# A two-layer transformer kernel: another split of its head's fills, loads and waits, and identity turns on PE at four seams

## The chip, the cores and the metric

The kernel is one program on one core of a Trainium2 chip, in one launch. The metric is the device time of that launch in microseconds (us), as the median of the runs shown. Engines: PE (TensorE), DVE (VectorE), ACT (ScalarE), POOL (GpSimd), SP (SyncE, which here only issues DMAs). PEld is PE's weight load.

## The reference, cut to what matters

Four sublayers on x of 4 batches x 512 rows x 256; each adds the layernorm of its result to x. The two feed-forward ones are mixtures of experts. All of it is float32.

```python
x = x + LN(attn0(LN(x), rms_w, wq, bq, wk, bk, wv, bv, wo, bo))   # 16 heads of 16, causal, rope
x = x + LN(moe0(LN(x), Wg, w1, w2))        # 8 experts, top 2, capacity 640, 256 -> 1024 -> 256
x = x + LN(attn1(LN(x), W_qkv, W_proj))    # 16 heads of 16, causal
x = x + LN(moe1(LN(x), gate_w, ...))       # 8 experts of width 128, top 2, computed for all rows, and a shared one

def _L0_attn_ref(x, ...):
    xn = x * rsqrt(mean(x * x) + 1e-5) * rms_w     # x is already LN(x): two norms in a row
    q, k, v = rope(xn @ wq + bq), rope(xn @ wk + bk), xn @ wv + bv
    return softmax(causal(q @ k.T / 4)) @ v @ wo + bo + x
```

## The kernel before, in words

The program is a row of phases, each a block of five instruction streams that ends when all five engines have come to its end: `setup_phase`, `norm_phase`, `attention_phase` of layer 0, `expert_phase` (about 320 to 552 us), `attention_phase` of layer 1, `dense_phase`. A row tile is 128 rows; a batch has four of them (`TPB`), so the 2048 rows are 16 tiles (`TILES`).

**Setup and norm.** In setup SP loads the first batch, the first weights (`EARLY`), then the other three batches and the second weights (`SECOND`: v, its bias, o and its bias, g). Meanwhile the three key stacks `k_st[0..2]` and query stacks `q_st[0..2]` are filled: zeros everywhere, and ones in the 32 rows of each head's slot. DVE does `k_st[0]` and the three `q_st`, the pads of v and the ones of `k_st[1]` (L1551); POOL zeroes `k_st[1]` and `k_st[2]`; ACT puts the ones of stacks 0 and 2 (L1538). Norm computes for the first batch the mean, `rstd` = (var+eps)^-1/2 and `rin`, the factor of both norms together, with two powers on POOL (L1595) in a row and three small DVE operations between and behind them. For tiles 4 to 15 the same is done within attention (`first_variance`, `first_square`, `first_scale` on DVE, `first_root` on POOL).

**Attention.** A batch's normalised rows are transposed on PE (L1034 for the first batch), scaled by ACT into `a_y_t` (L685), projected to q and k pieces (L993) and v (L1003). Each piece is split into a high part `a_hi` (ACT, `upper`, L697) and a low part `a_lo` (DVE or POOL); SP stores both to DRAM (`store_pieces`, L434 and L437) and loads them back as stacks (`load_stacks`, L456), four query and four key transfers for a group of four heads. PE then goes through 16 steps T, one for each batch and group of heads. A step has eleven places s, each with a max unit (L889: scores for the row maximum, which DVE takes in L1131) and a probability unit (L905) of an earlier step; values (L929) follow two steps behind. Other work of PE ("fills": transposes L985, projections, route logits L958, ranks L970 and L972) stands at places (T, s) that a planner has written out beforehand. DVE's small work for routing stands at places of its own: `weigh`, seven small operations that turn exponentials into gates and slots (L1284 to L1290), at (15, 6), at (16, 6) and once behind the loop.

The last batch of layer 0 goes through transposes of x ("rt", L985), logits (L958), `choose_top` (L1232 on) and the two rank products (L970, L972); POOL scatters its rows to the experts (`scatter`, L582); then the phase ends, and the experts' first act on PE is the transposes of L1846. Layer 1 starts with DVE joining the experts' results into x (L1349) with powers on POOL (`c_root`, L598), while ACT fills the stacks (L785 to L801), and PE's first work is L1034 again.

PE's clock has two levels in the profile, PEclk 0.50 and 1.00 (1.2 and 2.4 GHz).

## Time and profile before

| | |
|---|---|
| runs, us | 1045.17, 1049.98, 1049.54 (median 1049.54) |
| the profiled execution | 1050.82 us, of it a span of 1049.3 |
| mean granted clock of PE | 0.942 |
| busy share of the span | PE 88%, PEld 70%, DVE 58%, ACT 46%, POOL 42% |

The page's busy time is a sum over all phases: PE is busy through most of the span, and stands still at the start, at the two seams around the experts and in some holes. In its 40 slices PEclk drops at the same places.

### The profile page before, as it was taken

How to read it: one execution, taken by the hardware profiler on the slowest of the kernel's cores; microseconds unless marked ns; L12 is line 12 of the kernel's file. 1: busy time of each engine (PE TensorE's matmuls, PEld its weight loads, DVE VectorE, ACT ScalarE, POOL GpSimd, SP SyncE). 2: the span in 40 equal slices, each digit the busy share in tenths (PEclk: the TensorE clock that was granted, in tenths of full speed). 3: DMA queues.
4: the chain of work that ended last, by engine and by line, in shares of the span. 5: the costliest groups of instructions: out<-in, count | busy, mean ns of one | idle time of the engine just before them, and what ended most of it. 6: DMA issues, size and time to landing. Idle time of an engine off the chain costs nothing. (4 is left out here: it accounts for less than half of the span.)

```text
span 1049.3 us, 17283 instructions
## 1 busy us (share of the span) xinstructions
PE 926.2 (88%) x5776; PEld 730.8 (70%) x5776; DVE 610.6 (58%) x1983; ACT 486.2 (46%) x879; POOL 436.3 (42%) x410
## 2 busy tenths in 40 slices
PE   3799999998629999999990799999999789999997
PEld 1467766765418999999990456676767468888886
DVE  7577787878424444444444677786676335453535
ACT  2256566654304334333347164766666444343332
POOL 3443444514742233223335444555253544634233
PEclk9899999998858999999996799999999979999999
DMA  4543213210223333333114572533411010202111
GB/s 146 181 163 109 92 38 114 70 28 31 81 79 127 131 105 114 130 130 129 41 40 135 190 232 84 169 111 108 159 61 32 1 51 1 91 21 92 48 64 41
DMA packets 51966, 98.92 MB, mean 94 GB/s; under 512 B 7579, under 2 KB 23835, under 8 KB 51766
## 3 DMA queue, kind: packets, MB, share of 16 engines
q1 hardware_dynamic: 48822, 89.62, 25.2%
q0 software_dynamic: 3072, 8.39, 2.5%
q8 instruction: 38, 0.62, 0.3%
q14 instruction: 34, 0.28, 0.1%
HBM read 61.63 MB, written 36.36 MB: 93 GB/s over the span
## 5 line engine op out<-in xcount | busy, mean ns | idle before, releaser
L835 ACT ACTIVATE a_probs<-a_ps_b 128x512 f32<-128x512 f32 x320 | 187.6, 604 | 110.6 <-PE a_ps_b L905 107.9
L889 PE MATMUL a_ps_a<-a_k_st,a_q_st 128*128 128x256 f32 (+3 forms) x512 | 191.2, 421 | 16.4 <-DMA a_k_st<-scratch 8.9
L1131 DVE CUSTOM_DVE_ANT_0 a_masked_s<-a_ps_a,a_mask_f 128x512 f32<-128x512 f32 (+1 forms) x256 | 153.7, 621 | 85.6 <-PE a_ps_a L889 80.6
L517 POOL TENSOR_SCALAR_AFFINE_SELECT a_probs<-a_probs 128x512 f32<-128x512 f32 x128 | 80.5, 644 | 160.1 <-ACT a_probs L835 159.9
L889 PEld LDWEIGHTS a_ps_a<-a_k_st,a_q_st 128*128 128x128 f32 x512 | 95.7, 198 | 67.3 <-DVE a_nmax L1131 31.8
L905 PE MATMUL a_ps_b<-a_q_less,a_k_st 128*128 128x384 f32 (+3 forms) x512 | 134.1, 325 | 4.0 <-ACT a_probs L835 3.1
L1873 PE MATMUL exp_ps_o<-w_both,exp_h_hi 128*128 128x512 f32 x320 | 115.7, 402 | 0.0
L905 PEld LDWEIGHTS a_ps_b<-a_q_less,a_k_st 128*128 128x128 f32 x512 | 88.9, 191 | 29.3 <-ACT a_probs L835 17.6
L2020 POOL TENSOR_TENSOR dense_h_lo<-dense_mixed,dense_h_hi 128x512 fp32r<-128x512 f32 x40 | 53.0, 1326 | 101.8 <-ACT dense_h_hi L2085 101.8
L1791 ACT ACTIVATE exp_h_hi<-exp_ps_u 128x320 fp32r<-128x320 f32 x128 | 54.2, 438 | 87.4 <-PE exp_ps_u L1856 87.4
L1830 DVE SCALAR_TENSOR_TENSOR exp_h_lo<-exp_ps_u,exp_h_hi 128x320 fp32r<-128x320 f32 x128 | 61.5, 491 | 56.1 <-ACT exp_h_hi L1791 55.3
L929 PE MATMUL a_ps_pv<-a_probs,a_v 128*32 128x512 f32 (+3 forms) x1024 | 89.4, 459 | 1.6 <-POOL a_probs L517 1.6
L1875 PE MATMUL exp_ps_o<-w_both,exp_h_lo 128*128 128x256 f32 x320 | 89.8, 281 | 0.0
L1765 POOL TENSOR_TENSOR w_both<-w_raw,w_both 128x2048 fp32r<-128x2048 f32 x8 | 37.1, 4639 | 106.3 <-ACT w_both L1782 106.3
L1856 PE MATMUL exp_ps_u<-exp_x_t_hi,w_hi 128*128 128x320 f32 x256 | 80.0, 313 | 1.1 <-DVE exp_x_t_lo L1810 1.1
L1856 PE MATMUL exp_ps_u<-exp_x_t_hi,w_lo 128*128 128x320 f32 x256 | 79.7, 311 | 0.0
L1856 PE MATMUL exp_ps_u<-exp_x_t_lo,w_hi 128*128 128x320 f32 x256 | 79.7, 311 | 0.0
L2311 DVE TENSOR_TENSOR dense_product<-dense_gated,dense_ps_u 128x512 f32<-128x512 f32 x40 | 27.5, 688 | 74.8 <-PE dense_ps_u L2105 68.0
L1873 PEld LDWEIGHTS exp_ps_o<-w_both,exp_h_hi 128*128 128x128 f32 x320 | 60.1, 188 | 12.8
L2085 ACT CAST dense_h_hi<-dense_mixed 128x512 fp32r<-128x512 f32 x40 | 24.8, 620 | 83.5 <-DVE dense_mixed L2330 57.4
L1765 POOL TENSOR_TENSOR w_lo<-w_raw,w_hi 128x2048 fp32r<-128x2048 f32 x8 | 36.8, 4598 | 60.7 <-ACT w_hi L1782 60.7
L1875 PEld LDWEIGHTS exp_ps_o<-w_both,exp_h_lo 128*128 128x128 f32 x320 | 60.5, 189 | 0.0
(292 smaller groups left out, 2051.6 us busy)
## 6 DMA issues: line engine op xcount, KB each, us to landing
w_raw<-in_m_w SPq DMA_DIRECT2D x16, 1024.0 KB, 5.8
scratch<-a_hi SPq DMA_DIRECT2D x24, 512.0 KB, 3.0
dense_mix_rows<-mix_rows SPq DMA_DIRECT2D x9, 768.0 KB, 6.4
scratch<-a_lo SPq DMA_DIRECT2D x24, 256.0 KB, 3.4
a_q_st<-scratch SPq DMA_DIRECT2D x64, 96.0 KB, 2.2
a_k_st<-scratch SPq DMA_DIRECT2D x64, 96.0 KB, 2.4
exp_rows<-dispatched SPq DMA_DIRECT2D x9, 640.0 KB, 3.9
dispatched<-kept_sub SPq DMA_DIRECT2D x9, 512.0 KB, 3.0
```

The lines of the kernel that those rows point to most:

```text
L517: nc.gpsimd.affine_select(out=blocks, in_=blocks, compare_op=ALU.is_ge, fill=0.0, base=0, pattern=[[0, HPG], [1, P]], channel_multiplier=- ...
L835: nc.scalar.activation(probs[:, k, :], ps_b[k % B_BANKS][:, :], ACT.Exp, scale=scale).then_inc(exps, 1)
L889: last = nc.tensor.matmul(ps[:, at:at + wd], q_st[t % STACKS][:, h // PER_TILE, i * P:wd], k_st[t % STACKS][:, h, 0:wd], start=True, stop= ...
L905: last = nc.tensor.matmul(ps[:, at:at + wd], k_st[t % STACKS][:, h, j * P:(j + 1) * P], q_less[:, h // PER_TILE, j * P:SEQ], start=True, s ...
L929: last = nc.tensor.matmul(ps_pv[h * VW:(h + 1) * VW, at:SEQ], v[:, b % 2, j, g * HPG + h, :], rhs, start=(j == 0), stop=(j == 2), skip_gro ...
L1131: nc.vector.tensor_tensor_reduce(masked_s[n % 2][:, 0:wd], ps[:, 0:wd], mask_f[:, SEQ - wd:SEQ], -1.0, -NEG, ALU.add, ALU.min, nmax[:, t % ...
L1765: nc.gpsimd.tensor_tensor(of["lo"][:, :, :], of["raw"][:, :, :], of["hi"][:, :, :].bitcast(F32), ALU.subtract).then_inc(ready, 1)
L1791: nc.scalar.activation(h[0][:, f, half * HALF:(half + 1) * HALF], ps_u[n % U_BANKS][:, 0:HALF], ACT.Relu).then_inc(u_hi, 1)
L1830: nc.vector.scalar_tensor_tensor(h[1][:, f, cols], ps_u[n % U_BANKS][:, 0:HALF], 0.0, h[0][:, f, cols].bitcast(F32), ALU.max, ALU.subtract ...
L1856: last = nc.tensor.matmul(ps_u[(2 * f + half) % U_BANKS][:, 0:HALF], (w1["hi"], w1["lo"])[i][:, c, f * P:(f + 1) * P], x_t[j][:, c * CAP + ...
L1873: nc.tensor.matmul(bank[:, :], h[0][:, f, rows_at], w2["both"][:, f, :, :].rearrange("p k d -> p (k d)"), start=(f == 0), stop=False, skip ...
L1875: last = nc.tensor.matmul(bank[:, 0:D], h[1][:, f, rows_at], w2["hi"][:, f, :], start=False, stop=(f == FC - 1), skip_group_check=True)
```

## The change

1. **Head.** In setup only stack 0 is filled, SP loads two batches and `EARLY`, and POOL clears `sub` last. In norm ACT zeroes `k_st[1]` and `q_st[1]`, and SP issues the other seven loads. In attention ACT, behind its first two `a_y_t`, puts the ones of stack 1, fills stack 2, does `upper(0, 0)`, fills the pads of v, then `upper(0, 1)`.
2. **The two norms.** `rin` = ((1+eps) var + eps^2)^-1/2 in one power; `rstd`'s power for the first batch moves to POOL in attention. `first_variance` runs in two parts, tiles 4 to 7 and 8 to 15, each with its own semaphores and two powers.
3. **Stores and key waits.** The store of the high part waits for that part alone, that of the low part for both. At T = 0 each max unit waits for its own head's key transfer and no longer for all eight.
4. **Gates.** The first `weigh` moves from (15, 6) to (16, 3).
5. **Turns.** `turn_identity` transposes the 128x128 identity into a PSUM bank that nobody reads: 14 times in norm; in layer 0 12 times behind the first transposes, 30 before the loop, 36 before the last rt (behind a wait for the last exponential), 135 at the end; in layer 1 22 times at the start (behind a wait for the first power), 14 before the loop, 12 between the second and the third max unit.

```diff
+def turn_identity(nc, ps, ident, count):
+    for _ in range(count):
+        nc.tensor.transpose(ps[:, 0:P], ident[:, :], ident[:, :])
...
@@ store_pieces, load_stacks
-                sp.wait_ge(pieces, b * PT + (at + 1))
+                sp.wait_ge(hi_done, b * PT + (at + 1))
...
+                sp.wait_ge(pieces, b * PT + (at + 1))
                 sp.dma_start(scratch[b % 2, j, rest], lo[at % 2]...)
...
-                          .then_inc(stacked[t % STACKS], 16)
+                          .then_inc(first_keys[h] if t == 0 and which == 1 else stacked[t % STACKS], 16)
@@ POOL, layer 0
-                first_root(0)
+                nc.gpsimd.tensor_tensor(rstd[:, 0:TPB], rstd[:, 0:TPB], minus_half..., ALU.pow).then_inc(base_root, 1)
+                first_root(0, 0)
+                first_root(1, 0)
                 turn(0, 0)
                 lower(0, 0)
-                first_root(1)
                 for i in range(TPB):
                     normalise(1, i)
+                first_root(0, 1)
+                first_root(1, 1)
@@ ACT, layer 0
             for c in range(KC):
                 y_evac(0, c)
             if rope:
+                put_ones(1)
+                clear_stack(2, 1)
                 upper(0, 0)
+                clear_values(2 * TPB)
                 upper(0, 1)
@@ PE
+            if not rope:
+                pe.wait_ge(c_root[0], 1)
+                turn_identity(nc, ps_b[1], ident, 22)
...
+            if rope:
+                turn_identity(nc, ps_b[1], ident, 12)
...
+            turn_identity(nc, ps_b[1], ident, 30 if rope else 14)
...
+                        elif T == 0:
+                            turn_identity(nc, ps_b[1], ident, 12)
...
             for name in FINAL:
+                if name == ("rt", BATCH - 1, 0):
+                    pe.wait_ge(exps, STEPS * PROBS)
+                    turn_identity(nc, ps_b[1], ident, 36)
                 fill_whole(name)
+            if rope:
+                turn_identity(nc, ps_b[1], ident, 135)
@@ DVE, layer 0
                 first_rows()
+                first_stats(TPB, 2 * TPB).then_inc(n_chain[0], 1)
+                first_variance(0)
                 small_constants()
-                first_variance()
+                first_stats(2 * TPB, 3 * TPB)
                 ...
-                first_square()
...
-                first_scale()
+                first_stats(3 * TPB, TILES).then_inc(n_chain[1], 1)
+                first_variance(1)
...
-                    if rope and (T, s) in ((15, 6), (16, 6)):
-                        weigh(T - 15)
+                    if rope and (T, s) in ((16, 3), (16, 6)):
+                        weigh(s // 6)
@@ setup_phase
-            for b in range(1, BATCH):
-                load_rows(b)
-            for n in SECOND:
-                sp.dma_start(early[n].ap(), w[n]).then_inc(keep["early_in"][n], 16)
+            load_rows(1)
...
-            for i in (0, 2):
...
-            for i in range(STACKS):
-                nc.vector.memset(q_st[i][:, :, :].bitcast(F32), 0.0).then_inc(pads_zeroed, 1)
-            nc.vector.memset(v[:, :, :, :, HD:VW], 0.0).then_inc(pads_zeroed, 1)
...
-            for h in range(HPG):
-                nc.vector.memset(k_st[1][h * 32:h * 32 + 32, h, :].bitcast(F32), 1.0).then_inc(ones_put, 1)
+            nc.vector.memset(q_st[0][:, :, :].bitcast(F32), 0.0).then_inc(pads_zeroed, 1)
...
-            for i in (1, 2):
-                nc.gpsimd.memset(k_st[i][:, :, :].bitcast(F32), 0.0).then_inc(rows_zeroed[i], 1)
@@ norm_phase
+            turn_identity(nc, ps_idle, keep["ident"], 14)
...
+            for n in ("v", "bias_v"):
+                load_second(n)
+            for b in range(2, BATCH):
+                load_rows(b)
+            for n in ("bias_o", "o", "g"):
+                load_second(n)
...
+            nc.vector.tensor_scalar(var_rms[:, :], moments[:, :, 1], 1.0 + EPS, EPS * EPS, ALU.mult, ALU.add)...
+            nc.vector.tensor_scalar(rstd[:, lo:hi], moments[:, :, 1], EPS, None, ALU.add)...
-            after(nc.vector.tensor_tensor(mean_sq[:, :], moments[:, :, 1], rstd[:, lo:hi], ALU.mult))
-            after(nc.vector.tensor_tensor(mean_sq[:, :], mean_sq[:, :], rstd[:, lo:hi], ALU.mult))
-            nc.vector.tensor_scalar(var_eps[:, :], mean_sq[:, :], EPS, None, ALU.add).then_inc(var_ready, 1)
-            dve.wait_ge(root_ready, 2)
-            after(nc.vector.tensor_tensor(rin[:, lo:hi], rin[:, lo:hi], rstd[:, lo:hi], ALU.mult))
```

On ACT, from the end of setup to the second high part of layer 0, there stood before (branches between phases left out by "..."):

```order
L1538 CAST a_k_st<-kept_level 32x512 x8
...
L685 ACTIVATE a_y_t<-a_ps_m,early_rms_w 128x512 x2
L697 CAST a_hi<-a_part_q 128x512
L697 CAST a_hi<-a_part_k 128x512
L710 COPY a_v<-a_ps_m 128x32x16 x2
L746 ACTIVATE a_resid<-kept_x,kept_rstd 128x256 x4
```

and now, with the lines of the changed kernel (L815 puts ones, L806 and L807 fill, L820 and L823 fill the pads of v):

```order
L1572 CAST a_k_st<-kept_level 32x512 x4
...
L1641 CAST a_k_st<-kept_level 128x2048
L1642 CAST a_q_st<-kept_level 128x512
...
L702 ACTIVATE a_y_t<-a_ps_m,early_rms_w 128x512 x2
L815 CAST a_k_st<-kept_level 32x512 x4
L806 CAST a_k_st<-kept_level 128x2048
L807 CAST a_q_st<-kept_level 128x512
L815 CAST a_k_st<-kept_level 32x512 x4
L714 CAST a_hi<-a_part_q 128x512
L820 COPY a_v<-kept_level 128x16x16 x8
L823 COPY a_v<-kept_level 128x64 x2
L714 CAST a_hi<-a_part_k 128x512
```

Ten fills now stand between the second `a_y_t` and the first high part, and ten between the first and the second.

On PE, at the end of layer 0 (output projection, rt, logits, the two rank products, then the experts' first transposes), there stood before:

```order
L1003 MATMUL a_ps_m<-early_o,a_o_t 128x256 x8
L985 MATMUL a_ps_m<-kept_ident,kept_x 128x128 x8
L958 MATMUL a_ps_m<-a_w_gc,a_ry_t 128x8 x8
L970 MATMUL a_ps_m<-a_hot_sum,a_before 128x32
L972 MATMUL a_ps_m<-a_prior,a_ones 128x32
...
L1846 MATMUL exp_ps_t<-kept_ident,exp_rows 128x128 x10
```

and now:

```order
L1034 MATMUL a_ps_m<-early_o,a_o_t 128x256 x8
L45 MATMUL a_ps_b<-kept_ident 128x128 x36
L1016 MATMUL a_ps_m<-kept_ident,kept_x 128x128 x8
L989 MATMUL a_ps_m<-a_w_gc,a_ry_t 128x8 x8
L1001 MATMUL a_ps_m<-a_hot_sum,a_before 128x32
L1003 MATMUL a_ps_m<-a_prior,a_ones 128x32
L45 MATMUL a_ps_b<-kept_ident 128x128 x135
...
L1895 MATMUL exp_ps_t<-kept_ident,exp_rows 128x128 x10
```

The turns stand in the two places where PE had nothing queued, ahead of rt and behind the last rank product.

On DVE, in the step T = 15 of layer 0 (row maxima L1131, statistics L1185), the first `weigh` stood before as these seven rows:

```order
L1185 BN_STATS a_stats<-kept_sub 128x6
L1284 TENSOR_REDUCE a_total<-a_expd 128x4
L1285 RECIPROCAL a_inv_total<-a_total 128x4
L1286 TENSOR_TENSOR gates<-a_expd,a_inv_total 128x4
L1287 TENSOR_TENSOR gates<-a_expd,a_inv_total 128x4
L1288 TENSOR_TENSOR gates<-gates,a_fits 128x2x4
L1289 TENSOR_TENSOR a_slot<-a_slot,a_fits 128x2x4
L1290 CAST get_at<-a_slot 128x2x4
L1131 ISA a_masked_s,a_nmax<-a_ps_a,a_mask_f 128x384
```

and now stands in T = 16, behind the variance there (L1242) and right ahead of the second `weigh`:

```order
L1242 TENSOR_SCALAR a_var_eps<-a_moments 128x4
L1330 TENSOR_REDUCE a_total<-a_expd 128x4
L1331 RECIPROCAL a_inv_total<-a_total 128x4
L1332 TENSOR_TENSOR gates<-a_expd,a_inv_total 128x4
L1333 TENSOR_TENSOR gates<-a_expd,a_inv_total 128x4
L1334 TENSOR_TENSOR gates<-gates,a_fits 128x2x4
L1335 TENSOR_TENSOR a_slot<-a_slot,a_fits 128x2x4
L1336 CAST get_at<-a_slot 128x2x4
L1330 TENSOR_REDUCE a_total<-a_expd 128x4
```

The seven operations left the row of maxima that ends with `a_nm`, and stand behind it.

## Rows read from the trace of the kernel before

**Rows 1.** Waits of PE in the first 300 us: total, times, longest.

```profile
PE a_ps_m L918 <- DVE a_nm L1156: 6.7, 5, 3.5
...
PE a_ps_m L985 <- DVE kept_x L1204: 6.2, 1, 6.2
...
PE a_ps_a L889 <- DMA a_k_st<-scratch: 6.0, 1, 6.0
```

**Rows 2.** Windows: stretch, us; busy PE, PEld, DVE, ACT, POOL; PEclk, DMA share, GB/s.

```profile
16.11:38.73 22.62, 14.85 (x40) 8.27 (x41) 13.19 (x43) 5.17 (x10) 13.35 (x15) 0.98 0.26 91
...
38.73:47.95 9.22, 9.22 (x29) 6.68 (x30) 6.56 (x25) 1.37 (x2) 1.86 (x2) 0.50 0.65 222
...
253.20:259.30 6.10, 6.08 (x31) 2.85 (x32) 5.81 (x22) 0.72 (x2) 5.17 (x6) 0.50 0.13 46
...
295.60:313.04 17.44, 0.00 (x0) 0.00 (x1) 2.17 (x15) 0.00 (x0) 7.78 (x8) 0.50 0.28 98
...
313.04:321.00 7.96, 6.29 (x24) 5.52 (x25) 2.30 (x4) 2.04 (x5) 0.00 (x0) 0.50 0.81 296
...
577.20:583.80 6.60, 5.54 (x13) 3.12 (x14) 3.23 (x9) 1.07 (x2) 3.81 (x4) 0.50 0.27 79
```

**Rows 3.** Timeline, setup and norm: start, length, engine, what, idle before.

```profile
3.17 5.08 ACT L1538 CAST a_k_st<-kept_level 32x512 fp32r<-32x512 f32 x8 [0.86 <-DVE a_k_st L1542]
...
5.33 0.91 SPq L1527 DMA_DIRECT2D early_v<-in_a_v  x1
...
9.67 0.48 DVE L1551 MEMSET a_k_st<- 32x512 f32 x1 [0.16 <-issue]
...
12.58 1.02 POOL L1595 TENSOR_TENSOR kept_rstd<-norm_var_eps,kept_minus_half 128x4 f32<-128x4 f32 x1 [5.80 <-DVE norm_var_eps L1617]
...
15.40 0.16 DVE L1625 TENSOR_TENSOR kept_rin<-kept_rin,kept_rstd 128x4 f32<-128x4 f32 x1 [1.12 <-POOL kept_rin L1595]
...
16.58 1.57 PEld L1034 LDWEIGHTS a_ps_m<-kept_ident,kept_sub 128*128 128x128 f32 x8 [16.58 <-DVE kept_sub L1076]
```

**Rows 4.** Groups of ACT between 555 and 577: fills of layer 1.

```profile
L785 ACT CAST a_k_st<-kept_level 128x2048 fp32r<-128x2048 f32 x3 | 5.7, 1896 | 8.1 <-PEq L1668 8.1
...
L798 ACT COPY a_v<-kept_level 128x256 f32<-128x256 f32 x8 | 2.5, 398 | 0.0
```

**Rows 5.** Timeline, layer 0 up to its first keys.

```profile
18.44 1.27 ACT L685 ACTIVATE a_y_t<-a_ps_m,early_rms_w 128x512 f32<-128x512 f32 x2 [10.19 <-PE a_ps_m L1034]
...
27.83 0.62 ACT L697 CAST a_hi<-a_part_q 128x512 fp32r<-128x512 f32 x1 [8.12 <-POOL a_part_q L523]
...
30.77 0.62 ACT L697 CAST a_hi<-a_part_k 128x512 fp32r<-128x512 f32 x1 [2.33 <-DVE a_part_k L1100]
...
32.56 0.47 SPq L437 DMA_DIRECT2D scratch<-a_lo  x1
...
35.60 1.51 SPq L456 DMA_DIRECT2D a_k_st<-scratch  x4
```

**Rows 6.** Timeline of DVE, the first weigh and what follows it.

```profile
245.31 0.17 DVE L1284 TENSOR_REDUCE a_total<-a_expd 128x4 f32<-128x32 f32 x1
...
246.65 0.56 DVE L1131 CUSTOM_DVE_ANT_0 a_masked_s<-a_ps_a,a_mask_f 128x384 f32<-128x384 f32 x1
```

**Rows 7.** Transposes at the high clock: timeline of PE's weight loads.

```profile
273.39 0.86 PEld L985 LDWEIGHTS a_ps_m<-kept_ident,kept_sub 128*128 128x128 f32 x8 [1.18 <-issue]
```

**Rows 8.** One window of PE in which nothing but transposes ran.

```profile
835.00:836.00 1.00, 0.81 (x8) 1.00 0.00 0
```

**Rows 9.** Timeline, layer 0's last choice and layer 1's start.

```profile
292.12 0.19 DVE L1232 COPY a_logits<-a_ps_m 128x32 f32<-128x32 f32 x1 [0.88 <-PE a_ps_m L958]
...
571.74 1.67 DVE L1349 SCALAR_TENSOR_TENSOR kept_x<-kept_sub,a_c_inv,kept_x 128x256 f32<-128x256 f32 x4 [1.17 <-POOL a_c_inv L598]
...
577.22 1.94 PE L1034 MATMUL a_ps_m<-kept_ident,kept_sub 128*128 128x128 f32 x8 [24.35 <-DVE kept_sub L1076]
...
596.97 0.69 DVE L1131 CUSTOM_DVE_ANT_0 a_masked_s<-a_ps_a,a_mask_f 128x512 f32<-128x512 f32 x1 [0.26 <-DVE a_lo L1111]
```

More of the change, by code:

```diff
@@ L349, in attention_phase @@
         stacked = [sem(f"stacked{i}") for i in range(STACKS)]
+        first_keys = [sem(f"first_keys{h}") for h in range(HPG)]
         a_full, a_free, b_full, exps = sem("a_full"), sem("a_free"), sem("b_full"), sem("exps")
@@ L707, in v_evac @@
                 filled(act, name)
-                if not rope and b < 2 and i == 0:
+                if b < 2 and i == 0:
                     act.wait_ge(v_ready, 1)
@@ L743, in scaled @@
                 n = b * TPB + i
+                if b == 0 and i == 0:
+                    act.wait_ge(base_root, 1)
+                elif i == 0:
+                    act.wait_ge(n_root[min(b, 2) - 1], 2)
                 if b > 1:
@@ L791, in clear_stack, with clear_values @@
                     nc.scalar.copy(rows, keep["level"][base:base + SLOT, 1:2].to_broadcast([SLOT, SEQ])).then_inc(ones_in, 1)
-            if not rope:
-                clear_stack(0)
-                nc.scalar.copy(nm[:, :, :, :], level(0, nm[:, :, :, :])).then_inc(v_zeroed, 1)
+            def clear_values(count):
                 for b in range(2):
@@ L1029, in fill_whole @@
                     fill(name, part)
+            if not rope:
+                pe.wait_ge(c_root[0], 1)
+                turn_identity(nc, ps_b[1], ident, 22)
             for i in range(TPB):
@@ L1290, in weigh, with first_stats @@
                 after(nc.vector.tensor_copy(get_at[:, :, at], slot[:, :, at]))
-            def first_variance():
-                for n in range(TPB, TILES):
+            def first_stats(n0, n1):
+                for n in range(n0, n1):
                     if n % TPB == 0:
@@ L1509, in setup_phase @@
         filled, built = ctx.enter_context(nc.semaphore("filled")), ctx.enter_context(nc.semaphore("built"))
-        rows_zeroed = [ctx.enter_context(nc.semaphore(f"rows_zeroed{i}")) for i in range(STACKS)]
+        rows_zeroed = ctx.enter_context(nc.semaphore("rows_zeroed"))
         ones_put, pads_zeroed = ctx.enter_context(nc.semaphore("ones_put")), ctx.enter_context(nc.semaphore("pads_zeroed"))
-        q_st, k_st, v, nm = stacks["q_st"], stacks["k_st"], stacks["v"], stacks["nm"]
+        q_st, k_st, nm = stacks["q_st"], stacks["k_st"], stacks["nm"]
         block = ctx.enter_context(nc.Block())
@@ L1533, in _ @@
             act.wait_ge(keep["table_in"], 1)
[L1534 to L1538 removed]
+            act.wait_ge(rows_zeroed, 1)
+            for h in range(HPG):
+                rows = slice(h * 32, h * 32 + 32)
+                nc.scalar.copy(k_st[0][rows, h, :], keep["level"][rows, 1:2].to_broadcast([32, SEQ])).then_inc(ones_put, 1)
         @block.vector
         def _(dve):
[L1542 removed]
+            nc.vector.memset(k_st[0][:, :, :].bitcast(F32), 0.0).then_inc(rows_zeroed, 1)
             nc.vector.memset(nm[:, :, :, :].bitcast(F32), 0.0).then_inc(pads_zeroed, 1)
[L1544 to L1551 removed]
+            nc.vector.memset(q_st[0][:, :, :].bitcast(F32), 0.0).then_inc(pads_zeroed, 1)
         @block.gpsimd
@@ L2396, in program @@
                 setup_phase(nc, keep, io["x"], early, stacks, first)
-                norm_phase(nc, keep)
+                norm_phase(nc, keep, stacks, io["x"], early, first)
                 attention_phase(nc, keep, first, 0, route, w1, w2, early, stacks)
```

124 lines of the change are left out of this document (70 added, 54 removed).

## The prediction

> **What bounds the kernel now.** I read the page first: PE is the engine of the span, so only what PE waits for, or what it does at half clock, can be won. Then the waits of PE up to the experts [rows 1]: three holes of layer 0, 3.5 us (longest) for `a_nm`, 6.2 for the last batch's x, 6.0 for the first keys. Then windows around holes and seams [rows 2]. After each hole PEclk is 0.50 with PE nearly always busy: 9.22 of 9.22 us behind the first keys, 6.08 of 6.10 behind the `a_nm` hole, 5.54 of 6.60 at layer 1's start, 6.29 of 7.96 at the experts' start. So a hole costs twice, itself and the half clock behind it. Last, the timelines of the head [rows 3, 5]. The change touches the head (which bounds everything behind it, since every phase ends for all engines together), one hole and four seams; experts and dense layer stay.
>
> **Setup and norm.** Setup ends with DVE's last ones at 9.67 + 0.48 = 10.15 [rows 3]. Half of ACT's eight casts stay: 3.17 + 4 x 5.08/8 = 5.71. DVE and POOL keep less than that, so setup ends 4.44 earlier. In norm one power goes with its three DVE operations: the second power's product ends at 15.40 + 0.16 = 15.56, the first power at 12.58 + 1.02 = 13.60: 1.96, less 0.08 for one more small operation. That is 6.3 if DVE's chain still ends the phase, 9.2 on the new scale. But SP now issues seven loads there, which ran beside the fills before. One took 0.91 with the queue full [rows 3]; the stores and keys take 0.38 to 0.47 each [rows 5], so seven take 3.0 to 6.4, most likely 3.6, and SP, which starts them at about 6.0, ends at 9.0 to 12.4, most likely 9.6. I take 5.7, which leaves 0.6 for that (3.2 to 6.3). The first rows then start at 16.1 - 5.7 = 10.4. ACT's fill of `k_st[1]`, 1.90 [rows 4], and of the four times smaller `q_st[1]`, 0.5 by that, end at 8.5, beside the chain.
>
> **From the first rows to the first keys.** 22.62 us now [rows 2]. ACT ends its two `a_y_t` 3.60 behind the start of the rows (18.44 + 1.27 against 16.11) and starts the first high part at 11.72 [rows 5]: 8.1 idle. Into it go eight ones casts (2 x 2.54), one `k_st` (1.90) and one `q_st` fill (0.5) = 7.5: first high part at 11.1. It fits, if PE and DVE are not later; the 14 and 12 turns keep PE's clock, whose first transposes stood 1.57/8 = 0.196 apart [rows 3] against 0.86/8 = 0.107 at the high clock [rows 7], so the projections should come sooner, not later. Then the pads of v, 2.5 [rows 4] + about 0.5, then the second high part at 11.1 + 0.6 + 3.0 = 14.8 against 14.66. That is 0.1 lost, but the store of the high part no longer stands between the low part and its own store: the low store leaves at about 16.2, not 16.45. PE then needs one key transfer, not four: three times 1.51/4 = 1.1 [rows 5]. Together **1.3** (0.3 to 2.0; at the low end the fills push the second high part by a microsecond). Each microsecond by which the fills run over comes straight out of this term.
>
> **The half clock behind the first keys.** The 30 turns take 30 x 0.107 = 3.2 and stand in the 6.0 hole. In the 9.22 us at 0.50 DVE is busy 6.56, so at most 9.22 - 6.56 = 2.66 can go. PE waits for DVE inside each step then, its load halves, and the clock may well fall again. I take **0.7** (0 to 2.66), nearer the low end for that reason.
>
> **Gates.** 246.65 - 245.31 = 1.34 [rows 6] leave DVE's unbroken row before `a_nm`, for which PE waits 3.5 [rows 1]: the hole becomes 2.2. In their new place, in the next step, DVE no longer holds PE: there PE is busy 6.08 of 6.10 [rows 2]. Does the clock still fall? Now it is 0.50 for 6.1 us behind the hole [rows 2], which is worth up to 3.0. A hole of two thirds most often still drops it. I take **1.5** (1.3 to 4.3).
>
> **Layer 0's last batch.** 36 turns (3.9) stand in the 6.2 hole, so rt and the logits may run at full clock. The choice idles 0.88 for PE [rows 9], and DVE has other work up to then, so **0.7** (0 to 0.9) can go.
>
> **The 135 turns.** The hole behind the last product is 17.44 us [rows 2]. The first some twenty turns are still at half clock, 0.196 each, the others 0.107: 20 x 0.2 + 115 x 0.107 = 16.3. POOL's scatter ends the phase anyway; I price the overhang at 0.2 (0 to 0.4). Behind it the experts' first 7.96 us [rows 2] hold 6.29 of PE at half clock, but nothing is turned between the first rows, PE there waits for ACT and DVE, and the clock will fall again: **0.5** (0 to 3.1).
>
> **Layer 1's start.** The 22 turns are released by the power that ends before 571.74 [rows 9]; at 0.196 each they last 4.3 and end near 576.2, ahead of the rows that PE takes at 577.22 [rows 9]. If they raise the clock, the 5.54 busy us at 0.50 in the window 577.20 to 583.80 become 2.77. The loads, stores and DVE's lows follow, up to the first maximum at 596.97 [rows 9]: **2.75** (0.4 to 3.0). In its T = 0 the twelve turns (2.4 at half clock) stand where PE, with all three banks full, waits for the first maximum, by my estimate 1.3 (so up to 1.1 lost) against a gain as in layer 0: **0.6** (-1.1 to 2.0).
>
> **The sum.** 5.7 + 1.3 + 0.7 + 1.5 + 0.7 - 0.2 + 0.5 + 2.75 + 0.6 = 13.55. The profiled execution is 1050.8 (span 1049.3 and 1.5 around it), so 1037.3; it lies 1.3 above the median of the runs, 1049.54, so in their terms **1036.0**. About 7 of it come from the head's fills, loads and waits, 5.3 hang on the turns, 1.5 on the gates.
>
> **Do turns count for the clock?** Everything under the turns rests on that. In 835.00 to 836.00 PE did nothing but eight transposes, and the clock was 1.00 [rows 8]; it was so before, too, so the row shows a clock held, not one raised. The eight transposes at 577.22 ran at 0.50 [rows 2, 9], and none of these rows shows transposes alone raising it.
> The Trainium skill ("TensorE: Matmul & The Clock Gate", section "Part 4: PE-mode transpose") says the opposite: for transposes the clock gate's full level does not engage, since they don't count as PE being busy in the same way, and one costs about 275 ns. An estimate from its 275 ns: 135 turns would take 37 us, some 20 more than the hole holds, and the sum would turn into a loss. This case's row at 0.107 us for a transpose disagrees on the duration, and the row of 835 us on a held clock; on a raised one no row decides.
>
> **Rivals.**
> A, *the turns neither hold nor raise the clock* (slower). Place: the 135 turns at the end of layer 0. At 1.57/8 = 0.196 apart [rows 3] they last 26.5, against a hole of 17.4: +9.1; by the busy time of eight at half clock, 1.94/8 = 0.243 [rows 9], 32.8: +15.4. The 30 turns would last 5.9 to 7.3 against some 5: +0.9 to 2.3; the 12 in T = 0 +1.1. Head and gates still give 7.0 + 1.5. So +11.1 - 8.5 to +18.8 - 8.5, in terms of the runs 1052 to 1060, say 1056. It is slower from (17.4 + 8.5 - 2)/135 = 0.18 us a turn on. Against: [rows 7, 8]. 4 in 100.
> B, *the clock is raised, but given back where PE is half busy* (T = 0 of both layers, layer 1's start, the last batch): only head, gates and small change stay, 5.7 + 1.3 + 1.3 + 0.2 + 0.4 = 8.9: about 1041. For: PE's work in T = 0 is bounded by DVE, and the clock fell behind every hole. 18 in 100.
> C, *the clock stays up everywhere*: 2.66 and 2.0 in the T = 0s, 2 at the experts, together 4.9 more than in my sum, or the `a_nm` hole too no longer drops it: 1031 to 1029. 13 in 100.
> D, *SP's seven loads or ACT's fills become the head's bound*: norm ends at 12, the first keys come no earlier in their phase: the head gives 3, not 7: 1040. 10 in 100.
> The forecast has 55 in 100, with a range of its own of 1033 to 1039.
>
> **How the numbers follow.** The range runs from C's near end to B and D with a little room: 1029 to 1043. A and the tails lie outside. What a measurement of this kernel can tell is about 0.5%, 5.2 us: faster means below 1044.3. Forecast, B, C and D are all there, less a few chances that several low ends meet: faster 0.95. Same 0.02, slower 0.03, from A.
>
> **What would show it.** Right: the first rows near 10.4 us, the first max unit near 31.7; the hole of `a_nm` near 2.2; turns 0.107 apart, but for the first of the 135; the phase of layer 0 ending with POOL, not PE; PEclk 1.00 soon behind layer 1's first rows. Wrong: SP as the last engine of norm beyond 11; PE the last engine at layer 0's end, which would cost all by itself; clock at 0.50 in layer 1's projections; PE waiting for DVE in T = 16, where the gates went.

## The result, and the profile after

| | before | after |
|---|---|---|
| median of 8 runs, us | 1049.76 (1043.4 to 1055.8) | 1038.99 (1036.53 to 1043.49) |
| the profiled execution, us | 1050.82 (span 1049.3) | 1039.16 (span 1037.4) |
| mean granted clock of PE | 0.942 | 0.956 |

The ratio is 0.9906, with a 95% interval of 0.9879 to 0.9933: 10 to 11 us faster, against 13.55 predicted (1036.0 by time).

The waits of PE in the first 310 us of the changed kernel, in the columns of [rows 1]:

```profile
PE a_ps_m L949 <- DVE a_nm L1202: 6.0, 5, 2.8
...
PE a_ps_m L1001 <- DVEq L1308: 4.4, 1, 4.4
PE a_ps_a L920 <- DMA a_k_st<-scratch: 3.3, 1, 3.3
PE exp_ps_t L1895 <- DVEq L1853: 1.4, 1, 1.4
```

The hole of `a_nm` is 2.8 instead of 3.5; the 6.2 for the last batch's x are gone from the list, for the 36 turns stand in them, and of the 17.4 us ahead of the experts [rows 2] the barrier alone is left (1.4).

The windows that answer to [rows 2], on the new time scale, and then PE alone in the 135 turns, with the durations of single ones (shortest, median and longest, in ns):

```profile
9.76:31.95 22.19, 18.46 (x83) 13.71 (x83) 12.18 (x43) 15.01 (x30) 14.71 (x17) 1.00 0.42 145
31.95:39.85 7.90, 7.90 (x29) 5.80 (x29) 5.95 (x25) 1.37 (x2) 2.62 (x3) 0.57 0.48 151
245.74:252.00 6.26, 6.24 (x35) 2.92 (x35) 5.98 (x23) 1.17 (x3) 5.17 (x6) 0.59 0.12 42
288.90:306.65 17.75, 16.33 (x137) 16.11 (x138) 2.18 (x15) 0.00 (x0) 7.78 (x8) 0.92 0.27 98
306.65:314.60 7.95, 5.79 (x25) 5.18 (x26) 2.27 (x5) 2.32 (x5) 0.00 (x0) 0.64 0.81 298
571.17:575.80 4.63, 3.47 (x13) 2.07 (x14) 3.32 (x9) 1.09 (x3) 3.71 (x4) 0.95 0.27 76
```

```profile
288.90:291.80 2.90, 2.90 (x16) 0.50 0.03 6
291.80:305.20 13.40, 13.40 (x123) 1.00 0.35 124
...
L45 PE MATMUL a_ps_b<-kept_ident x123: 272/273/418, 291.5 to 305.0; 128*128 128x128 f32 x123
```

Behind the first keys, behind the `a_nm` hole and at the experts' start the clock fell all the same (0.57, 0.59, 0.64): there the turns or the shorter hole did not hold it. At layer 1's start it is 0.95 instead of 0.50. And the two windows of the turns answer what no row of before could: PE had been idle and at 0.50, did nothing but transposes of the identity, and the clock rose to 1.00. Transposes count, against the rule of the Trainium skill that the prediction quoted ("TensorE: Matmul & The Clock Gate", section "Part 4: PE-mode transpose"). On the duration the prediction misread its own row: 0.107 us is the distance between two starts (0.109 here), while a single turn lasts 0.273 in the median (last row). With that the 275 ns of the same section agree; what fails is the estimate of 37 us for 135 turns, which took the 275 ns for the distance.

The head's timeline, answering to [rows 3] and [rows 5]:

```profile
3.16 2.53 ACT L1572 CAST a_k_st<-kept_level 32x512 fp32r<-32x512 f32 x4 [0.86 <-DVE a_k_st L1576]
5.96 0.33 SPq L1629 DMA_DIRECT2D early_v<-in_a_v  x1
8.11 1.02 POOL L1648 TENSOR_TENSOR kept_rin<-norm_var_rms,kept_minus_half 128x4 f32<-128x4 f32 x1 [4.81 <-DVE kept_rstd L1672]
8.85 0.43 SPq L1629 DMA_DIRECT2D early_g<-in_m_g  x1
9.76 1.38 DVE L1122 TENSOR_SCALAR kept_sub<-kept_x,kept_mean,kept_rin 128x256 f32<-128x256 f32 x4 [1.59 <-PEq L1602]
...
20.75 0.62 ACT L714 CAST a_hi<-a_part_q 128x512 fp32r<-128x512 f32 x1
24.14 0.61 ACT L714 CAST a_hi<-a_part_k 128x512 fp32r<-128x512 f32 x1
25.24 3.44 PE L45 MATMUL a_ps_b<-kept_ident 128*128 128x128 f32 x30
25.50 0.32 SPq L447 DMA_DIRECT2D scratch<-a_lo  x1
25.87 3.01 SPq L467 DMA_DIRECT2D a_q_st<-scratch  x4
30.03 1.51 SPq L467 DMA_DIRECT2D a_k_st<-scratch  x4
31.95 2.56 PE L920 MATMUL a_ps_a<-a_k_st,a_q_st 128*128 128x512 f32 x5 [3.26 <-DMA a_k_st<-scratch]
```

SP issued its seven loads from 5.96 to 9.28, and DVE's chain ended at 9.13 with the power, so SP can have held the phase by 0.15 at most; the first rows start at 9.76, not 10.4. The first high part starts 10.99 behind them (11.1 predicted), the second 14.38 (14.8). The first max unit comes at 31.95 (31.7 predicted). ACT's fills end at 20.62, 0.1 before the product that the first high part takes (POOL, 20.72): they fit, as predicted.

**Where the time went.** I took the start of the same instruction of DVE in two traces and subtracted. A plus is time won since the mark above; "predicted" is the term of the sum.

| from mark to mark (start in before) | predicted | after | where it stands alone |
|---|---|---|---|
| start to the first rows (16.11) | 5.7 | 6.36 | 6.35 (e2) |
| to the first maximum (39.53) | 1.3 | 0.72 | 1.43 (e10: waits), -0.65 (e2: the new head) |
| to T = 0's end (47.32) | 0.7 | 0.41 | 0.07 (e4), 0.01 (e10) |
| to 245 | 0 | -1.39 | +0.05 (e3), -1.24 (e4, e10) |
| over the first weigh's old place (252.9) | 1.5 | 1.36 | 1.36 (e3) |
| to the last batch's x (284.71) | 0 | -1.96 | +0.3 (e5, e6) |
| to its choice (292.12) | 0.7 | 0.97 | 0 without the 36 (e5) |
| to 340.5, in the experts | 0.3 | -0.30 | -0.88 without the 135 (e5) |
| to layer 1's first rows (576.66) | 0 | -0.23 | |
| to its first low part (584.61) | 2.75 | 2.26 | 0.27 without the 22 (e6) |
| to its T = 0's end (606.8) | 0.6 | 0.84 | 0.82 without the 12 (e6) |
| to the end, by the time of the execution | 0 | 2.62 | |
| sum | 13.55 | 11.66 | |

The eight rows with a term add up to 12.6 of the 13.55, and four stretches in which nothing was changed but when they start give and take -1.4, -2.0, -0.2 and +2.6.

### The profile page after: what moved, and what is told of

Read it like the earlier page. It is cut to its first block and busy times, and to the rows that moved or that the text cites. A ratio compares the mean times of both kernels' runs of the same rounds, so it can differ in the third digit from the quotient of the medians.

```text
span 1037.4 us, 17851 instructions
## 1 busy us (share of the span) xinstructions
PE 956.2 (92%) x6051; PEld 762.9 (74%) x6051; DVE 603.9 (58%) x1972; ACT 495.6 (48%) x897; POOL 434.3 (42%) x410
## 5 line engine op out<-in xcount | busy, mean ns | idle before, releaser
L960 PE MATMUL a_ps_pv<-a_probs,a_v 128*32 128x512 f32 (+3 forms) x1024 | 92.2, 472 | 1.6 <-POOL a_probs L529 1.6
L960 PEld LDWEIGHTS a_ps_pv<-a_probs,a_v 128*32 128x32 f32 x1024 | 27.0, 115 | 49.1 <-issue 40.6
```

What stands on the lines that cost most here:

```text
L960: last = nc.tensor.matmul(ps_pv[h * VW:(h + 1) * VW, at:SEQ], v[:, b % 2, j, g * HPG + h, :], rhs, start=(j == 0), stop=(j == 2), skip_gro ...
```

## The experiments

The runs of a kernel and of before stood on the same chip in each group. Ratios are to before in that group, with 95% intervals. e1 to e4 ran on a chip where before took 1059.52 (35 runs); e5 to e8 where it took 1048.48; e9 to e12, 1049.32.

| | kernel | median | ratio (interval) |
|---|---|---|---|
| e1 | changed, no turns | 1052.37 | 0.9937 (0.9914 to 0.9960) |
| e2 | head's fills, loads and root alone | 1055.40 | 0.9954 (0.9933 to 0.9976) |
| e3 | gates alone | 1056.00 | 0.9972 (0.9951 to 0.9994) |
| e4 | turns alone | 1056.37 | 0.9970 (0.9950 to 0.9990) |
| e5 | changed, without 36 and 135 | 1038.47 | 0.9917 (0.9889 to 0.9945) |
| e6 | changed, without 22, 14, 12 | 1038.57 | 0.9898 (0.9864 to 0.9932) |
| e7 | changed, more turns | 1034.58 | 0.9861 (0.9823 to 0.9900) |
| e8 | e7 and the experts' first rows | 1033.83 | 0.9866 (0.9827 to 0.9905) |
| e9 | e8 and the seam to dense | 1031.05 | 0.9818 (0.9770 to 0.9865) |
| e10 | store and key waits alone | 1049.30 | 0.9993 (0.9965 to 1.0021) |
| e11 | changed, 200 instead of 135 | 1045.51 | 0.9956 (0.9928 to 0.9984) |
| e12 | e9 and layer 0's last batch | 1033.98 | 0.9835 (0.9791 to 0.9880) |

**e1: the changed kernel without turns**

```diff
-                pe.wait_ge(c_root[0], 1)
-                turn_identity(nc, ps_b[1], ident, 22)
...
-                turn_identity(nc, ps_b[1], ident, 135)
...
-            turn_identity(nc, ps_idle, keep["ident"], 14)
```

> The changed kernel without any turn of the identity (head, stores, key waits and gates as changed). Theory, the turns pay by the clock: 5.3 us of the gain go, so about 1044 against 1039.0 of the changed kernel and 1049.8 before; layer 1's projections (8 of 512 columns) again 0.85 us apart for the first four, the last batch's logits again 0.22 apart, the experts' first rows cold. Rival, the turns only fill time that was idle anyway and the gain is the head's: 1039, with the same phase lengths. Rival, the turns cost at layer 0's end: below 1039.

Measured: 0.63% faster than before, 6.7 us, which leaves 3.3 us of the 0.94% for the turns. As a difference of two ratios that is good to some 3.7 us only (estimated from the two intervals), so by itself it shows neither the 5.3 forecast nor that turns pay at all; e4 does. The head of e1, up to its first keys:

```profile
10.23 1.97 PE L1067 MATMUL a_ps_m<-kept_ident,kept_sub 128*128 128x128 f32 x8 [10.23 <-DVE kept_sub L1111]
13.49 9.92 PE L1024 MATMUL a_ps_m<-a_y_t,early_qk 128*128 128x512 f32 x16 [1.30 <-ACT a_y_t L702]
...
22.21 0.62 ACT L714 CAST a_hi<-a_part_q 128x512 fp32r<-128x512 f32 x1 [1.58 <-POOL a_part_q L535]
...
31.52 2.86 PE L920 MATMUL a_ps_a<-a_k_st,a_q_st 128*128 128x512 f32 x5 [4.65 <-DMA a_k_st<-scratch]
```

The 16 projections take 9.92 us and end at 23.4; in the changed kernel they start a microsecond later, behind the 12 turns, take 7.41 and end at 22.0. Without turns ACT stands idle for 1.58 ahead of the first high part (22.21), so it is PE's projections that set it, by way of POOL's product, and not ACT's fills. With them both high parts start 1.5 earlier, at 20.75 and 24.14 instead of 22.21 and 25.59, and the last low store leaves at 25.50 instead of 26.96. Yet the first keys come at 31.52, if anything before those of the changed kernel. What was won is gone between that store and the key transfers (30.03 in the changed kernel, 29.70 here), which wait until the store has landed. From issue to landing it took, in the changed kernel and in before:

```profile
scratch<-a_lo SPq DMA_DIRECT2D x1, 256.0 KB, 4.5
...
scratch<-a_lo SPq DMA_DIRECT2D x1, 256.0 KB, 3.0
```

The other profiles show how much this varies. In the eight kernels that have the head's turns the first max unit starts 19.9 to 22.2 us behind the first rows, and the changed kernel's profile is the latest of them; here it is 21.76. So the head's turns moved the projections by 1.5, and by the first keys that was worth between -0.4 and 1.9. Why the landing varies was not tried.

**e2: the head alone** (against the changed kernel; all turns are out too)

```diff
-                sp.wait_ge(hi_done, b * PT + (at + 1))
+                sp.wait_ge(pieces, b * PT + (at + 1))
...
-                    if n < HPG:
-                        pe.wait_ge(first_keys[h], 16)
...
-                    if rope and (T, s) in ((16, 3), (16, 6)):
-                        weigh(s // 6)
+                    if rope and (T, s) in ((15, 6), (16, 6)):
+                        weigh(T - 15)
```

> Setup, norm, ACT's order and the folded root as changed; key waits, store waits and gates as before, no turns. Theory: 5.7 to 6.3 from setup and norm; without the single key transfer and the early low store nothing behind it, or a loss of 0.1 to 1 by ACT's fills: 1043.5 to 1044.5, first rows at 9.8 and the first max unit 5.5 to 6.5 earlier than before. Rival, what is won at the head is lost again at holes behind it where the clock falls at another place: within 2 us of before by time, though the first max unit is 6 earlier.

Measured: 4.9 us faster (2.5 to 7.1). Rows 6.35 earlier, first maximum 5.70, so 0.65 is lost behind the rows. The second high part starts 15.40 behind them instead of 14.66; 0.34 of that is ACT's pads of v, which end that much after its input is ready (25.17 against 24.83), and about as much is PE, whose 16 projections took 9.49 instead of 9.19.

```profile
33.03 2.35 PE L917 MATMUL a_ps_a<-a_k_st,a_q_st 128*128 128x512 f32 x4 [6.58 <-DMA a_k_st<-scratch]
```

Against e1's 31.52 the store and key waits are worth 1.51.

**e3: the gates alone**

```diff
-                    if rope and (T, s) in ((15, 6), (16, 6)):
-                        weigh(T - 15)
+                    if rope and (T, s) in ((16, 3), (16, 6)):
+                        weigh(s // 6)
```

> The kernel before with the first weigh moved from (15, 6) to (16, 3) alone. Theory as predicted: the wait of PE for a_nm shrinks from 3.5 to 2.2 and the kernel gains 1.3 to 1.5, about 1048.3. Rival, from the trace after: the wait shrinks only to about 2.8, since PE itself comes later or DVE's row waits elsewhere, and later places give it back: 0 to 0.7.

Measured: 3.0 us (0.6 to 5.2). At the place itself 1.36, the duration of the seven operations to 0.02. The largest wait for `a_nm` is 2.6 in its trace instead of 3.5:

```profile
PE a_ps_m L918 <- DVE a_nm L1156: 5.9, 5, 2.6
```

The wait shrinks by less than the gain, since PE too comes to it earlier: DVE's unbroken row holds its maxima as well. The rival read the size of the wait, and the wait is the wrong measure.

**e4: the turns alone**

```diff
+            turn_identity(nc, ps_b[1], ident, 30 if rope else 14)
...
+                turn_identity(nc, ps_b[1], ident, 135)
```

> The kernel before with the identity turns of the attention phases alone (12, 30, 36, 135 in layer 0; 22, 14, 12 in layer 1; not the 14 in norm). Theory: minus 4 to 5.5, about 1045; the phase of layer 0 ends with POOL. Rival, turns are no activity for the clock: 135 turns of 0.2 to 0.24 us, layer 0 ends 9 to 15 us later, 1060 or more. If e1 and e4 both show the turns' gain, it is independent of the head.

Measured: 3.1 us faster (1.1 to 5.3). Rival A is out. Turns are worth 3.1 without the head and 3.3 with it, the latter loosely; the parts add up within that.

**The chip of e1 to e4.** All four lose 7 to 10 us between 264 and 285 against the profile of before, mostly in three stretches of 2.0 to 5.0 us in which PE stands still while ACT or DVE waits for something that the trace puts to no engine of the core ("remote"). They are in e1:

```profile
ACT a_pv_sb L873 <- remote: 6.5, 1, 6.5
DVE a_picked L1304 <- remote: 3.4, 1, 3.4
ACT a_o_t L739 <- remote: 2.1, 1, 2.1
```

No profile of before was taken on that chip, but before was 10 us slower there too. What holds the engines there stays open; stage by stage I use these four only up to 258 and behind 285.

**e5: without the turns at layer 0's end**

```diff
-                if name == ("rt", BATCH - 1, 0):
-                    pe.wait_ge(exps, STEPS * PROBS)
-                    turn_identity(nc, ps_b[1], ident, 36)
-            if rope:
-                turn_identity(nc, ps_b[1], ident, 135)
```

> The changed kernel without the 36 and the 135 turns at the end of layer 0; all others stay. Theory, by the sum (0.7 + 0.5 - 0.2) and by the trace after (the last batch's logits 0.97 and the experts' start 0.4 earlier): 1 us slower than the changed kernel, a ratio to before of 0.9915. Rival, the 135 turns' warm clock holds on into the experts' first matmuls: 2 to 3 slower. Rival, they delay the barrier: faster by up to 0.4.

Measured: no difference by time (1038.47 against 1038.99). By trace the 0.97 at the last choice is gone, as expected; and up to there this kernel is the changed one, instruction for instruction. Yet its last output projection ran at full clock:

```profile
268.00 3.69 PE L1034 MATMUL a_ps_m<-early_o,a_o_t 128*128 128x256 f32 x16 [1.01 <-ACT a_o_t L739]
```

and in the changed kernel the same 16 matmuls took 6.11:

```profile
269.80 6.11 PE L1034 MATMUL a_ps_m<-early_o,a_o_t 128*128 128x256 f32 x16 [0.87 <-ACT a_o_t L739]
```

In the same code with the same waits the clock fell at 267.9 in one execution and stayed up in the other. DVE's first take of the result stands at 270.00 against 273.59: 3.6 us, of which 0.6 had come before 245.

**e6: without layer 1's turns**

```diff
-                turn_identity(nc, ps_b[1], ident, 22)
...
-            turn_identity(nc, ps_b[1], ident, 30 if rope else 14)
+            if rope:
+                turn_identity(nc, ps_b[1], ident, 30)
...
-                            turn_identity(nc, ps_b[1], ident, 12)
```

> The changed kernel without the 22, 14 and 12 turns of layer 1. Theory, by the sum (2.75 + 0.6) and by the trace after (3.9 won between the start of layer 1's rows and its first keys): 3.3 to 3.9 slower than the changed kernel, ratio 0.994. Rival, half of it is given back at the next hole: 1.5 slower. The last turns before layer 1's first rows gone, PE's first transposes stand 0.196 apart and the first four projections 0.85.

Measured: by time no difference (0.9898 against 0.9906). By trace 2.0 are missing between rows and first low part (0.27 against 2.26), none behind it:

```profile
568.86 1.94 PE L1067 MATMUL a_ps_m<-kept_ident,kept_sub 128*128 128x128 f32 x8 [24.59 <-DVE kept_sub L1120]
571.85 5.20 PE L1024 MATMUL a_ps_m<-a_y_t,a_w_qk 128*128 128x512 f32 x8 [1.04 <-ACT a_y_t L704]
```

In the changed kernel:

```profile
565.91 4.93 PE L45 MATMUL a_ps_b<-kept_ident 128*128 128x128 f32 x22 [19.22 <-POOL a_c_inv L611]
571.18 1.46 PE L1068 MATMUL a_ps_m<-kept_ident,kept_sub 128*128 128x128 f32 x8 [0.34 <-DVE kept_sub L1122]
573.79 3.67 PE L1024 MATMUL a_ps_m<-a_y_t,a_w_qk 128*128 128x512 f32 x8 [1.15 <-ACT a_y_t L704]
```

So 22 turns bought 0.5 in the transposes and 1.5 in the projections. The 12 within T = 0 and the 14 ahead of it bought nothing: e6 wins the same 0.82 there. The 3.3 to 3.9 of the theory were 2.0 at the place.

**e7: more turns**

```diff
+                ps = bank(name)
+                if rope and t == STEPS - 1 and n == 0:
+                    turn_identity(nc, ps, ident, 24)
...
-            turn_identity(nc, ps_b[1], ident, 30 if rope else 14)
+            turn_identity(nc, ps_b[1], ident, 52 if rope else 14)
```

> The changed kernel with 24 more turns in the bank of a_nm's transposes, in the hole of T = 15, and 52 instead of 30 before the loop of layer 0. Theory, a hole costs itself and the half clock behind it: behind the a_nm hole PE stays at 1.00, up to 3 us by the 6.1 us at 0.50; T = 0 starts at 1.00 instead of 0.50 for its first 4.7 us, up to 1: together 2 to 4 faster than the changed kernel, ratio 0.987. Rival, what is won in PE is DVE's and ACT's to give there (DVE busy 4.30 of 4.60 us, POOL's powers): 0 to 1. If both holes stay at 0.50 behind them, turns ended too early.

Measured: 1034.58, 4.4 under the changed kernel; the ratio's interval (to 0.9900) still overlaps that of after. In the trace the 24 turns end as the wait ends,

```profile
242.09 2.78 PE L45 MATMUL a_ps_m<-kept_ident 128*128 128x128 f32 x24
244.96 0.66 PE L951 MATMUL a_ps_m<-a_identr,a_nm 128*128 128x128 f32 x4
```

the four transposes behind them take 0.66, not 1.08, and the clock does not fall there: from 252.9 to the third batch's logits (267.76 in before) 3.3 us are won, where the changed kernel lost 0.6. The 52 turns before the loop brought no more in T = 0 (0.38) than the 30 did (0.41). Layer 1's start in the same trace shows the other side, in windows (columns as in [rows 2]) of the 22 turns, the rows and the first projections:

```profile
559.68:564.20 4.52, 4.52 (x22) 4.52 (x22) 3.56 (x15) 3.38 (x6) 3.08 (x3) 0.50 0.20 58
564.95:567.50 2.55, 1.46 (x8) 0.81 (x8) 2.44 (x8) 1.07 (x2) 1.94 (x3) 1.00 0.16 51
567.56:572.80 5.24, 5.24 (x9) 2.23 (x10) 1.49 (x3) 0.59 (x1) 1.89 (x2) 0.67 0.28 81
```

The turns raised the clock, and it fell again in the row's own holes: 0.57 won there, not 2.26. In e8, the same code 1.2 us earlier, it stayed:

```profile
558.51:563.40 4.89, 4.89 (x22) 4.52 (x22) 3.65 (x16) 3.41 (x6) 3.33 (x3) 0.50 0.21 57
563.78:566.30 2.52, 1.47 (x8) 1.08 (x8) 2.41 (x8) 1.07 (x2) 1.91 (x3) 0.88 0.16 52
566.39:570.00 3.61, 3.61 (x9) 1.67 (x10) 1.49 (x3) 0.58 (x1) 1.88 (x2) 1.00 0.37 110
```

**e8: and between the experts' first rows**

```diff
             for fill in range(T_FILLS):
                 transposes(0, 0, fill)
+                if fill > 0:
+                    turn_identity(nc, ps_u[0], ident, 9)
```

> The kernel of e7 with 9 turns each behind the second and third fill of the experts' first rows, in a bank that the first matmul then overwrites. Theory: the clock, which fell again at 308 us, stays up over the first matmuls of 320 columns: 1 to 1.5 faster than e7. Rival, each nine turns last longer than the wait for the copies (0.96 and 1.19), or the phase is bound by the weights' loads anyway: same or 0.5 slower.

Measured: by time 1033.83, not told apart from e7. By trace: from the last choice to 340.5 this kernel wins 1.5 on before where after lost 0.3 and e7 won 0.3. The window from the first rows:

```profile
302.00:310.00 8.00, 7.87 (x58) 7.43 (x59) 3.32 (x7) 3.19 (x7) 0.00 (x0) 1.00 0.80 295
```

1.00 all through, against 0.64 in the changed kernel.

**e9: and the seam to the dense layer**

```diff
+                if name in (("ot", BATCH - 1, 0), ("out", BATCH - 1, 0)) and not rope:
+                    pe.wait_ge(exps, STEPS * PROBS)
+                    turn_identity(nc, ps_b[1], ident, 7)
...
-            if rope:
-                turn_identity(nc, ps_b[1], ident, 135)
+            turn_identity(nc, ps_b[1], ident, 135 if rope else 18)
```

> The kernel of e8 with 7 turns each ahead of the last output transposes and the last output projection of layer 1, and 18 behind them. Theory, holes at the seam to the dense layer drop the clock (in e8 it fell at 824 and ran at 0.50 to 830 us): the gates' first products at full clock, 2 to 3.4 faster than e8, ratio 0.984 or less. Rival, the clock falls at one of the next holes instead and the gain is given back there: 0 to 1.

Measured: 1031.05, ratio 0.9818, the fastest version by its median: 18 us under before and clearly faster than the changed kernel (its interval ends at 0.9865, where after's begins at 0.9879). From e8 it is not told apart, since those intervals overlap. In its trace the seam is at full clock, 810 to 835, and in e8's at 0.84:

```profile
810.00:835.00 25.00, 21.27 (x153) 16.86 (x152) 8.13 (x38) 10.07 (x16) 11.68 (x14) 1.00 0.16 54
```

```profile
810.00:835.00 25.00, 19.59 (x113) 14.55 (x113) 7.55 (x35) 8.83 (x14) 11.66 (x14) 0.84 0.15 54
```

The turns cost 1.4 ahead of the seam (by 842), and 3.3 are won by 857. But the profile of before has a fall of the clock at 843 there, and the changed kernel, with no turn at this seam, wins the same 3.3 there; e12 has the same turns, loses 4.2 by 842 and wins nothing by 857. So the seam's turns are not shown to be what made e9 fast.

**e10: the store and key waits alone**

```diff
-                sp.wait_ge(pieces, b * PT + (at + 1))
+                sp.wait_ge(hi_done, b * PT + (at + 1))
...
+                    if n < HPG:
+                        pe.wait_ge(first_keys[h], 16)
```

> The kernel before with the store waits and the single key waits of the change alone. Theory, by the sum (0.2 for the low store, 1.1 for three key transfers) and by e1 against e2 (first max unit 7.21 against 5.70 earlier): 1.3 to 1.5 faster than before, ratio 0.9987, first max unit at 37.2 to 37.4 instead of 38.7. Rival: the wait of PE in T = 0 passes to the next unit's keys: 0.

Measured: 0.9993, with an interval (0.9965 to 1.0021) that holds both. By trace the first max unit starts at 37.30 instead of 38.73, 1.43 as the theory had it:

```profile
37.30 2.35 PE L893 MATMUL a_ps_a<-a_k_st,a_q_st 128*128 128x512 f32 x4 [4.00 <-DMA a_k_st<-scratch]
```

1.24 of them are gone by 213, where the clock fell once more than in before. That place comes back below.

**e11: 200 turns**

```diff
-                turn_identity(nc, ps_b[1], ident, 135)
+                turn_identity(nc, ps_b[1], ident, 200)
```

> The changed kernel with 200 instead of 135 turns at the end of layer 0. Theory: 65 more turns at 0.107 last 7.0, of which 1.4 lie in the hole that was left behind the 135: PE ends layer 0, 5.5 us later, about 1044.5; so the 135 are free and the hole's length is the limit. Rival A, turns at half clock: 65 x 0.2 = 13 and 1050 or more. In either case PE, not POOL, is the last engine of the phase.

Measured: 1045.51, 6.5 over the changed kernel; 1 more than expected.

```profile
286.95 23.49 PE L45 MATMUL a_ps_b<-kept_ident 128*128 128x128 f32 x200
311.87 1.07 PE L1895 MATMUL exp_ps_t<-kept_ident,exp_rows 128*128 128x128 f32 x8 [1.43 <-DVEq L1853]
```

The 1.4 us behind the 135 turns that I had taken for room are the barrier: they stand behind the 200 as well. So all 65 turns were paid, some 7 us, and every turn more costs its full 0.109. The 135 end just when the phase would have ended without them: the first rows come 5.76 us behind POOL's last scatter, and 5.75 in e5, which has no turns there. In e6 and e7, where more of the 135 ran at half clock, it is 6.5: there they cost 0.7.

**e12: and layer 0's last batch**

```diff
-                if name in (("ot", BATCH - 1, 0), ("out", BATCH - 1, 0)) and not rope:
+                if name in (("ot", BATCH - 1, 0), ("out", BATCH - 1, 0)):
```

> The kernel of e9 with 7 turns each ahead of the last output transposes and projection of layer 0 too. Theory: the last batch's output projection, at half clock in the changed kernel (16 matmuls in 6.11 us instead of 3.69) and in part in e8, keeps the full clock: up to 2 faster than e9. Rival, that row of waits is DVE's and ACT's, and e8 already had the projection at full clock by its second half: 0 to 0.5. Candidate for the fastest version.

Measured: 1033.98 (0.9791 to 0.9880), not told apart from e9. By trace it won 0.9 more up to the last batch's x, and then had its clock fall at 801 for 14 us and three times more by 870; e9's fell for 3 us at 801 and then not before 955. Nor does the place bear the theory out: from 252.9 to the last batch's x it wins 3.0 on before, and e7 and e8 win the same 3.0 without these turns; only e9 falls short of it (2.3), by a longer fall of the clock, from 262 to 269.

**The same stretches in all profiles** (us won on before, as in the table of marks):

| stretch of before | with the edit | without it |
|---|---|---|
| gates, 245 to 252.9 | 1.35 to 1.37, ten profiles | 0.00, three |
| 24 turns ahead of `a_nm` (e7, e8, e9, e12), 252.9 to 267.8 | 3.33 or 3.34, four | -0.59 to 0.34, nine |
| 36 turns, 284.7 to 292.1 | 0.88 to 0.97, eight | 0.00 to 0.28, five |
| 135 turns, 292.1 to 340.5 | -0.74 to 0.26, four | -0.88 to -0.09, five |
| these and 9 turns twice (e8, e9, e12), the same stretch | 1.55 to 2.01, three | |
| 22 turns, 576.7 to 584.6 | 2.26 in seven, 0.57 in one | 0.00 to 0.27, five |

Within its own stretch each of these edits but the 135 turns stands clear of the profiles without it. There is also one loss that comes back. Every kernel with a turn or the new waits ahead of it (eleven profiles) loses 1.60 to 1.64 between 205 and 213, and the three without (before, e2, e3) lose nothing. PE waits 1.0 us for `a_nm` there in all of them. Behind this wait the clock stays at 1.00 in before and goes to 0.50 in the changed kernel:

```profile
210.10:214.10 4.00, 3.94 (x35) 2.20 (x34) 1.96 (x7) 1.19 (x3) 0.00 (x0) 1.00 0.27 68
...
202.40:206.40 4.00, 4.00 (x26) 1.69 (x29) 1.13 (x4) 0.58 (x1) 0.00 (x0) 0.58 0.25 64
```

Why it falls in the eleven and not in the three is not shown. It takes back all that e4 had won by then, and all but 0.2 of what e10 had.

## Why the prediction held, point by point

**The head.** Setup 4.44 and norm 1.9 came as worked out. My own deduction of 0.6 for SP was wrong: its loads took 0.33 to 0.51 each, 3.3 in all, and ended 0.15 behind DVE's chain. Shown by the timeline.

**First rows to first keys.** 0.72 instead of 1.3. Stores and key waits bring 1.4 to 1.5 (e10; e1 against e2), as predicted, and the new head alone costs 0.65 (e2), where I had 0.1; about half of it is ACT's pads. The two nearly add up to 0.72, but by luck: the changed kernel has its turns too, which moved both high parts 1.5 forward (e1), and lost that again to a low store that took 4.5 us to land instead of 3.0, and to SP's four query transfers, which took 3.01 instead of 1.97. I had no term for either.

**The half clock behind the first keys.** Mis-sized: 0.41 in the trace, and by e1 and e4 the turns' share is 0.1 to 0.3. The 30 turns ended at 28.7, and the keys came at 31.95; with 52 turns (e7) the clock stayed up to 35 us instead of 32 and still fell. Rival B was right for this place.

**Gates.** 1.36 of 1.5, and alone (e3). The hole itself shrank to 2.8 or 2.6, not to the 2.2 that I had named as the sign.

**Layer 0's last batch.** 0.97, shown by e5, over the top of my range by 0.1. The clock fell at 284.9 only.

**The experts' start.** The one term that came with the wrong sign, though small: forecast +0.3 (0.5 less the overhang of 0.2), measured -0.30. In this profile the overhang of the 135 turns is nil, but the clock fell at 308.8, between the first rows, and came back at 315.7. Against e5 (-0.88) the 135 bring 0.6; over all profiles the ranges with and without them overlap, and by time e5 is as fast, so that they pay is not shown. The sign "layer 0 ends with POOL, not PE" failed narrowly too: PE's last turn ends at 305.23 and the experts' first transposes start 1.43 behind it, in e11 as well. It could be won with turns between the rows: e8.

**Layer 1.** 2.26 instead of 2.75, and 2.0 of it by the 22 turns (e6), or all of it by the other kernels without them. The 0.6 of its T = 0 came, 0.84, but not by the turns: e6 has it too, so that term was right by its number and wrong by its cause.

**What I had left out.** I counted a clock term at each place as if the rest of the kernel kept its clock. It doesn't keep it alike in every execution: in 22 runs of before in one group the time goes from 1044.8 to 1056.8 and the mean clock from 0.952 to 0.935, with a correlation of -0.96; in 35 on the slower chip the same -0.96. This kernel has a dozen holes, of which some let the clock fall in one execution and others in the next. In the changed kernel's profile that cost 2.0 before 285 and gave 2.6 behind 607: 1.5 by 650, where before's clock fell at 635 and this one's did not, and 1.5 at the seam to dense, where before ran at 0.50 from 843 to 850 us and the changed kernel earlier, from 811 to 824. A profile is one draw of this. The 1.4 lost before 245 are another matter: they are the 1.6 at 205 to 213, which every kernel with turns or the new waits pays, and I had no term for them. That the sum came within 1.9 of the profiled 11.66 is in part luck: the stretches that I had not priced, up to 2.6 each, happen to cancel to -1.0.

**The rivals.** A is out (turns 0.107 apart, clock raised by turns alone, e4 faster). B held for both T = 0s, for layer 1's start in one profile of eight (e7), and not for the last batch. C held nowhere in the changed kernel; e9 comes to C's time with more turns, though its clock still falls in eight places. D did not come.
